# A fifth pair of a row by seven products, U1 summed in its PSUM bank, and the shared output added to x in DRAM

## What is computed

```
mlp(x, g, u, d) = (gelu(x @ g) * (x @ u)) @ d          # g, u: 256 x 1024, d: 1024 x 256
y = x + mlp(x, shared) + sum over the 2 chosen of 8 experts e: w[b, e] * mlp(x, skill[e])
out = y + y @ W_base.T + b_base + 2 * sum over e: cond[b, e] * (y @ A[e].T) @ B[e].T
```

## Time and profile before

| | us |
|---|---|
| median of 3 runs | 797.29 |
| lowest, highest | 796.95, 797.66 |
| the profiled execution | 796.85 |
| its span, first to last instruction | 795.0 |
| busy: TensorE (PE), its weight loads (PEld) | 789.5, 681.1 |
| busy: DVE, ACT, POOL | 668.8, 478.5, 278.4 |

### The profile page before, as it was taken

How to read it: one execution, slowest core, us unless ns; L and a number is a source line. 1 busy time by engine, 2 the same in 40 slices (tenths; PEclk the granted TensorE clock), 3 DMA queues, 4 the chain that set the end, 5 groups by cost and what they waited for, 6 DMA issues and landing times.

```text
span 795.0 us, 13413 instructions
## 1 busy us (share of the span) xinstructions
PE 789.5 (99%) x4133; PEld 681.1 (86%) x4133; DVE 668.8 (84%) x910; ACT 478.5 (60%) x737; POOL 278.4 (35%) x284
## 2 busy tenths in 40 slices
PE   8999999999999999999999999999999999999998
PEld 7888888888888888888888889888898888898887
DVE  4866888888887899889888898888898889889886
ACT  6554564564664666656666666666666666566653
POOL 1621321321430363263352444425435234532520
PEclk9999999999999999999999999999999999999999
DMA  7436506304726632563563275346336426631400
GB/s 204 123 80 200 144 1 198 121 1 146 233 72 206 222 116 80 171 184 101 165 189 95 90 224 153 105 141 189 106 125 215 124 80 198 172 108 51 133 2 27
DMA packets 138894, 105.21 MB, mean 132 GB/s; under 512 B 62928, under 2 KB 131280, under 8 KB 138832
## 3 DMA queue, kind: packets, MB, share of 16 engines
q1 hardware_dynamic: 138832, 104.53, 43.7%
HBM read 79.86 MB, written 24.64 MB: 131 GB/s over the span
## 4 chain that ended last, share of the span: by engine, by line
PE 99%; DMA 0%; DVE 0%; ACT 0%; SPq 0%; DVEq 0%; issue 0%
PE ps_ring L827 61%; PE ps_acc L827 36%; DMA raw<-_L_cond_shared_gate_dram 0%; PE ps_acc L1039 0%; PE ps_ring L848 0%; PE ps_ring L853 0%; PE ps_ring L857 0%; PE ps_acc L1059 0%; DVE stage L1925 0%; PE ps_acc L944 0%; PE ps_ring L1059 0%; ACT xc L1165 0%; PE ps_acc L1085 0%; ACT wide L1165 0%; SPq L517 0%
## 5 line engine op out<-in xcount | busy, mean ns | idle before, releaser
L827 PE MATMUL ps_ring<-xc,wide 128*128 128x512 f32 (+1 forms) x1926 | 416.2, 364 | 0.0
L827 PEld LDWEIGHTS ps_ring<-xc,wide 128*128 128x128 f32 x1926 | 336.8, 189 | 59.4 <-DVE post L1568 0.6
L1165 ACT CAST inner_hi<-post 128x512 fp32r<-128x512 f32 x192 | 117.7, 621 | 102.9 <-DVE post L1857 31.8
L827 PE MATMUL ps_acc<-inner_hi,wide 128*128 128x512 f32 x504 | 171.0, 390 | 0.0
L1511 DVE TENSOR_TENSOR inner_lo<-post,inner_hi 128x512 fp32r<-128x512 f32 x192 | 146.3, 769 | 9.0 <-ACT inner_hi L1165 6.1
L1168 ACT ACTIVATE post<-ps_ring 128x512 f32<-128x512 f32 (+1 forms) x125 | 68.0, 546 | 103.4 <-PE ps_ring L827 98.0
L827 PEld LDWEIGHTS ps_acc<-inner_hi,wide 128*128 128x128 f32 x504 | 94.8, 188 | 19.1
L827 PE MATMUL ps_acc<-inner_lo,wide 128*128 128x512 f32 x252 | 98.4, 391 | 0.0
L1168 ACT ACTIVATE post<-post 128x256 f32<-128x256 f32 (+1 forms) x98 | 53.7, 563 | 53.4 <-DVE post L1798 36.3
L827 PE MATMUL ps_acc<-inner_hi,sh_dn 128*128 128x512 f32 x256 | 83.9, 389 | 0.0
L1857 DVE SCALAR_TENSOR_TENSOR post<-post,coef_now,ps_ring 128x512 f32<-128x512 f32 x66 | 49.3, 747 | 36.2 <-PE ps_ring L827 34.1
(11 more groups left out here) (126 smaller groups left out, 1015.5 us busy)
## 6 DMA issues: line engine op xcount, KB each, us to landing
rights_scratch<-xc SPq DMA_DIRECT2D x6, 1792.0 KB, 10.2
raw<-n_L_cond_skill_gate_dram SPq DMA_DIRECT2D x32, 256.0 KB, 3.0
raw<-in_L_cond_skill_up_dram SPq DMA_DIRECT2D x32, 256.0 KB, 3.5
raw<-n_L_cond_skill_down_dram SPq DMA_DIRECT2D x32, 256.0 KB, 3.9
xbuf<-n_L_cond_skill_gate_dram SPq DMA_DIRECT2D x32, 256.0 KB, 3.0
xbuf<-in_L_cond_skill_up_dram SPq DMA_DIRECT2D x32, 256.0 KB, 3.5
xbuf<-n_L_cond_skill_down_dram SPq DMA_DIRECT2D x32, 256.0 KB, 3.8
xt_scratch<-xbuf SPq DMA_DIRECT2D x8, 512.0 KB, 3.3
```

The source lines that it names most:

```text
L827: last = pe.matmul(dst, left_[a], right_[b], start=start and n == 0, stop=stop and n == len(PASSES) - 1, skip_group_check=adds)
L1165: return nc.scalar.copy(dst, src)
```

## The change

- `SEVEN` becomes 1, 3, 5, 6, 7 and `FIRST_SEVEN` 3, 5, 6, 7: pairs 5, 6 and 7 stand next to one another.
- ACT copies bank 0 (P1) into bank 1, and the fourth product accumulates there; the finished U1 is copied to SBUF by ACT. DVE's addition at L1791 goes.
- For pairs by seven, block A21 of gate and up is not split any more (5/6 of the columns), the raw layout is regrouped for it. DVE's split of such a pair waits until POOL has read the slot.
- The `lo` parts of two steps are taken in one instruction where no pair by seven follows directly, else one by one within the next pair.
- x is stored to both `xt_scratch` and a new `base_scratch`; POOL adds the shared output to the latter with two accumulating transfers a quarter (`add_shared`). The row sum on POOL and SP's wait for it go. SP's loads and stores are reordered in a row.
- The orders by step are rewritten: down products of a pair behind a pair by seven go together after its second step, layer 1 is at step 5 in place of 4.
- Five transposes of the identity are added on TensorE between the first x transposes and the first unit.

```diff
...
-    L1_STEP = 4
+    L1_STEP = 5
     CONST_STEP = 3
     BW_STEP = 5
-    COEF_STEP = 13
+    COEF_STEP = 9
     FOLD_STEP = 8
     W_EFF_STEP = 9
-    W_EFF_FIRST_STEP = 10
-    W_EFF_LO_STEP = 12
+    W_EFF_LO_STEP = 2
     X_STEP = 8
-    TURN_STEP = 4
-    SEVEN = [1, 3, 5, 7]
+    LATE_STEP = 9
+    X1_LO_STEP = 4
+    TURN_STEP = 6
+    SEVEN = [1, 3, 5, 6, 7]
     FIRST_SEVEN = SEVEN[1:]
+    WHOLE_FIRST = len(SEVEN) - len(FIRST_SEVEN)
...
+        SPLIT_FIRST = {0: 2, 2: 3, 4: 4, 6: 5, 9: 6, 14: 9}
+        SPLIT_LATER = {1: 2, 4: 3, 5: 4, 6: 5, 9: 6, 14: 9}
+        SPLIT_WITHIN = {10: 7, 14: 8}
+        SPLIT_BEHIND = {10: 7}
+        SUMS_FIRST = {5: 1, 8: 2, 9: 3, 12: 4}
+        SUMS_LATER = {0: 0, 4: 1, 8: 2, 9: 3, 12: 4}
...
-                sp.dma_start(xt_dram[2 * qn + r], xbuf[:, r * 2 * S:(r + 1) * 2 * S]).then_inc(xt_stored[r], 16)
...
+                for to in (xt_dram, base_dram):
+                    sp.dma_start(to[2 * qn + r], xbuf[:, r * 2 * S:(r + 1) * 2 * S]).then_inc(xt_stored[r], 16)
...
+                    tokens(b)
+                    load_routed(b, 1, range(2, 3))
+                    sp.wait_ge(ex_s_made, 1)
+                    load_routed(b, 1, range(3, 4))
+                    load_routed(b + 1, 0, range(0, 2))
                 else:
+                    if not last:
+                        tokens(b)
+                    load_routed(b, 1, range(2, 3))
                     sp.wait_ge(x1_ready, b)
                     sp.wait_ge(sh_stored, 16 * B)
-                    sp.dma_start(base, sh_dram[b]).then_inc(base_landed, 16)
-                load_routed(b, 1, range(2, PAIRS))
+                    sp.dma_start(base, base_dram[b]).then_inc(base_landed, 16)
+                    load_routed(b, 1, range(3, 4))
+                    if not last:
+                        load_routed(b + 1, 0, range(0, 1))
+                    store_blocks(b - 1)
+                    if not last:
+                        load_routed(b + 1, 0, range(1, 2))
                 if not last:
-                    sp.wait_ge(base_ready, b + 1)
-                    sp.wait_ge(x_ready, b + 1)
-                    sp.dma_start(xf, xt_dram[b + 1]).then_inc(xf_landed, 16)
-                    load_routed(b + 1, 0, range(0, 1))
-                if not first:
-                    store_blocks(b - 1)
-                if not last:
-                    load_routed(b + 1, 0, range(1, PAIRS))
+                    load_routed(b + 1, 0, range(2, PAIRS))
                     load_routed(b + 1, 1, range(0, 2))
+            def tokens(b):
+                sp.wait_ge(x_ready, b + 1)
+                sp.dma_start(xf, xt_dram[b + 1]).then_inc(xf_landed, 16)
...
+            def add_shared(q):
+                for r in range(2):
+                    pool.wait_ge(xt_stored[r], 32 * (q + 1))
+                pool.wait_ge(acc0_out, 2 * (q + 1))
+                to, what = shared_place(q, 0)
+                pool.dma_start(to, what, accum_op=ALU.add).then_inc(sh_stored, 16)
+                pool.wait_ge(acc1_out, 2 * (q + 1))
+                to, what = shared_place(q, 1)
+                pool.dma_start(to, what, accum_op=ALU.add).then_inc(sh_stored, 16)
...
-                pool.wait_ge(weights_ready, b * (TOP_K * PAIRS) + (SEVEN[n_s - 1] + 1 if n_s else 0))
-                v = raw_gu(j).rearrange("p (g c i) -> p g c i", g=2, c=HC)
+                if not (b_first and SEVEN[n_s] == FIRST_SEVEN[0]):
+                    pool.wait_ge(ex_s_split, st)
...
             def row(b, first, last):
                 if first:
+                    add_shared(Q - 1)
                     pool.wait_ge(sh_stored, 16 * B)
-                    sums_of_weights(b, 1)
-                    row_sum(b)
-                    ex_c22(b, 1)
-                    sums_of_weights(b, 2)
+                    sums_of_weights(b, 1, True)
                 else:
                     sums_of_weights(b, 1)
                     ex_c22(b, 0)
-                    row_sum(b)
-                    sums_of_weights(b, 2)
-                    ex_c22(b, 1)
+                sums_of_weights(b, 2)
+                ex_c22(b, 1)
                 sums_of_weights(b, 3)
+                sums_of_weights(b, 4)
                 ex_c22(b, 2)
+                ex_c22(b, 3)
                 if not last:
                     sums_of_weights(b + 1, 0)
-                ex_c22(b, 3)
+                ex_c22(b, 4)
...
+            for _ in range(5):
+                pe.transpose(ring[3][:, 0:P], ident[:], ident[:])
...
+                    if n == 1:
+                        pe.wait_ge(ex_s_split, st + 1)
+                        if first:
+                            pe.wait_ge(ex_t_ready, 1)
+                    if n < 3 and k // 2 - 1 in sevens_of(first):
+                        pe.wait_ge([ex_mul, ex_c_done, ex_c_done][n], [3 * st - 2, 2 * st - 1, 2 * st][n])
+                    elif n == 0:
                         pe.wait_ge(gelu_done, whole(b, k - 1, first))
                     elif n == 1:
-                        if first:
-                            pe.wait_ge(ex_t_ready, 1)
                         pe.wait_ge(mul_done, whole(b, k - 1, first))
                     elif n == 2:
                         pe.wait_ge(mul_done, whole(b, k, first))
                     elif n == 3:
-                        pe.wait_ge(gelu_done, whole(b, k, first))
+                        pe.wait_ge(ex_copied, 2 * st + 1)
                     elif n in (4, 5):
                         pe.wait_ge(ex_copied, 2 * st + n - 3)
                     else:
                         pe.wait_ge(ex_v_done, st + 1)
                     for part in (GATE, UP):
                         last = product(ring[bank][:, part * HS:(part + 1) * HS],
-                                       [ex_left(n_s, hl, part, a_) for hl in range(2)],
+                                       [ex_left(par, n_s, hl, part, a_) for hl in range(2)],
                                        [ex_right(par, hl, b_) for hl in range(2)],
-                                       opens and part == GATE, True, True)
+                                       opens and part == GATE and n != 3, True, True)
...
-                    if k < 2 and not first:
-                        down(b - 1, K - 2 + k, False)
+                    if k == L1_STEP and not first:
+                        layer1(b - 1)
+                    if k == 1 and not first:
+                        down(b - 1, K - 2, False)
+                        down(b - 1, K - 1, False)
                     if k == 2:
                         pe.wait_ge(acc0_out, 2 * Q)
-                    if k >= 2:
+                    if k >= 2 and k // 2 - 1 not in sevens_of(first):
                         down(b, k - 2, first)
-                    if k == L1_STEP and not first:
-                        layer1(b - 1)
+                    elif k > 2 and k % 2 == 1:
+                        down(b, k - 3, first)
+                        down(b, k - 2, first)
...
+            def ex_copy_out(b, k, n_s, first):
                 st = seven_no(b, n_s)
+                behind_seven = k // 2 - 1 in sevens_of(first)
+                if behind_seven:
+                    ex_inner_hi_of(b, k - 2, n_s - 1, 0)
                 if first and SEVEN[n_s] == FIRST_SEVEN[0]:
                     act.wait_ge(turned_w, 1)
                     act.wait_ge(a_ready, 1)
-                elif n_s == 1:
+                act.wait_ge(ex_product, st * NP + 1)
+                if behind_seven:
+                    act.wait_ge(ex_u1_done, st)
+                else:
+                    act.wait_ge(gelu_done, whole(b, k, first))
+                nc.scalar.copy(ring[1][:], ring[0][:]).then_inc(ex_copied, 1)
+                if behind_seven:
+                    ex_inner_hi_of(b, k - 2, n_s - 1, 1)
+                act.wait_ge(ex_product, st * NP + 2)
+                act.wait_ge(ex_mul, 3 * st)
+                nc.scalar.copy(ex_v, ring[2][:]).then_inc(ex_copied, 1)
+            def ex_copy_u1(n_s, b):
+                st = seven_no(b, n_s)
+                if SEVEN[n_s] == L1_STEP // 2 + 1:
                     act.wait_ge(o_ready, b * 2)
-                for n, to, bank in ((0, ex_u1, 0), (1, ex_v, 2)):
-                    act.wait_ge(ex_product, st * NP + n + 1)
-                    if n == 0:
-                        act.wait_ge(ex_mul, 3 * st)
-                    nc.scalar.copy(to, ring[bank][:]).then_inc(ex_copied, 1)
+                act.wait_ge(ex_product, st * NP + 4)
+                nc.scalar.copy(ex_u1, ring[1][:]).then_inc(ex_u1_done, 1)
...
+            def split_routed(b, s, j, seven, first=False):
                 dve.wait_ge(weights_hi, b * (TOP_K * PAIRS) + PAIRS * s + j + 1)
-                last = take_lo(ex_all(1, j), raw[j], ex_all(0, j))
-                if not sums_follow:
-                    last.then_inc(weights_ready, 1)
+                if seven:
+                    if not first:
```

(33 more changed lines are left out.)

247 lines of the change are left out of this document (132 added, 115 removed).

## The result

The changed kernel takes **806.77 us** (median of four runs, 806.09 to 809.66), the kernel before took 797.35 beside it: a ratio of 1.0125 with a 95% interval of 1.010 to 1.0151, slower by 9.4 us. The forecast was 794.4. The profiled execution of the changed kernel is its longest, 809.66 us with a span of 807.8; the other three are 2.5 to 3.6 us shorter, so that the losses by place, which are read from this longest one, add up to more than those of the median.

What follows compares the result with a forecast made beforehand. TensorE's instruction count times pitch was taken as the bound, other engines hidden. Span 795.0 - 3.04 + 0.2 = 792.2, with 1.85 around it 794.0, plus 0.44 for the median: 794.4 us; range 793.3 to 797.6.

Steps and rivals of the forecast that it cites:

- rival B: Row 0 and shared quarters: accumulating transfers landing after 14 us lose 4 and 2 each, 804 us; decides from 12; chance 0.06.
- Eight pairs, 3.04 us: TensorE, one more pair by seven products in each row: eight pairs each 0.38 us shorter, 3.04 us off.
- E: Pairs by seven save nothing because narrow matmuls behind narrow ones wait for their weights: 797 us; chance 0.03.
- D: Columns alone set TensorE's pace, so narrow matmuls shrink with them: eight pairs save 5.4 us, 792 us; chance 0.02.
- Transposes 0: Kernel start: five more transposes fill TensorE's 0.6 us wait for the first x block; cost 0, bounds -0.1 to +0.1.
- U1 in its bank: ACT's copy into bank 1 takes 0.57 us, bounds to 1.3, ready 0.6 us before the fourth product; DVE's addition goes.
- Loads: Other engines' work in a row: DVE about -0.7 us from 59.1, ACT +4 from 42.8, POOL less; none near 66.8.
- The timetable: Adjacent pairs 5, 6, 7 and the next row's start: least slack 0.6 us, mostly 1.0; cost 0.
- C22 stands behind pair 7's sums: POOL's queue at pair 5: C22 ends at 6.9 us, pair 7's weights ready at 9.8, wanted at 15.5.
- Moved waits 0: SP's reordered stores and loads, DVE's pair 6 split waiting for POOL, layer 1 one step later: cost 0.
- Accumulating transfers 0: Shared output on POOL's queue: landing 4.5 to 9 us, against about 10 allowed in row 0 and 12 in quarters; cost 0.
- Plain stores at the start: Two x stores ahead of the third pair's shared weights delay them 3.4 us against 3.3 slack: 0.2 us, bounds 0 to 1.5.

Runs made afterwards that it cites:

- the repaired kernel: Changed kernel with plain SP stores, x added later in DRAM, ACT's and DVE's rows written out, no five transposes, C22 before pair 7's sums: 794.72 us.

## Why the prediction was wrong

The verdict went to rival B, the accumulating transfers, at 0.06, with a part that stood under no rival.

1. **Eight pairs, 3.04 us: right.** Rows of 66.83 to 66.85 where nothing waits, pairs of 7.77 to 7.79. Matmuls behind matmuls of 256 columns keep the 0.120 us of the earlier trace rows, so E and D fall, and with D the Trainium skill's 2.5 ns fixed part (TensorE: Matmul & The Clock Gate, section "Wait — 56ns, not 53.3ns?"), which this trace again does not show.
2. **Transposes 0: right** by the median; up to 0.64 in a profile.
3. **U1 in its bank: right.** The copy into PSUM took 0.57 to 0.58 us and was 0.6 ahead. What I did not see is how much it holds up (19 us).
4. **Loads: right in that none comes near the row's length.** In rows without waits DVE has 55.5 to 57.1 us of 66.85, where the sum gave 58.4, ACT 43.6 to 45.6 (46.8) and POOL 27.9 to 29.8 (26).
5. **The timetable: right inside the later rows, where TensorE waits for nothing, and incomplete in two ways.** I had written it for a later row and applied it to row 0, where pair 7's sums start 3.0 us into pair 5 and C22 behind them ends at 8.5: some 0.7 us lost, 0.4 of it given back by C22's earlier place, in the step "C22 stands behind pair 7's sums". And it took the row's beginning as step 14's remainder alone. It left out the turn of DVE's loop, which no wait of TensorE before named, because it was covered: DVE was idle there for 1.04 us at 453.32 (behind ACT's turn), while in the middle of the loop it was 0.50. With the row's work ending later, DVE's turn reaches pair 1's third product: 2.6 to 3.1 us over rows 3 and 5, and 4.9 in the profile of the changed kernel. **This was missed altogether.**
6. **Moved waits 0: half wrong.** I counted what stands in front of SP's stores and not what had stood behind the shared ones: 1.5 MB that now go out first and share the engines, 5 of the 13.2 us.
7. **Accumulating transfers 0: wrong, and the step that decided.** The bound "9 us, each byte read and written" was right for the median (8.0) and was taken for all places; in row 0 it was 13.2, past the 10 us of slack. There the wait and its clock cost 5.25 us. And in the quarters the test was wrong: I asked whether ACT would be kept waiting and found 12 us, but not what POOL's work would run beside once it was late. It ran beside DVE's, at 1.77 us for 0.68, and cost 3.8 us with the transfer well inside the slack. Even in row 0 the slack was less than I had it, for at 8.7 us TensorE already waited. Rival B's price (row 0: 4, three quarters: 2 each, 804) was close to the 5.25 and 3.8, its condition of 12 us too high: the quarter lost at 9.3. POOL's issues took 1.0 to 2.0 us as bounded, 0.55 to 0.94 when plain: it was not the issue that hurt but the landing. The Trainium skill (SBUF — State Buffer, section "SBUF: two separate sides") says that a POOL-issued transfer of 620 ns takes 3100 beside a copy of DVE, since its descriptors are not written while DVE holds the shared port. I had weighed this, and no run here shows how much of a landing is such a wait.
8. **Plain stores at the start: right in effect**, TensorE waited for nothing behind them. The working was off: 1 MB at 223 GB/s takes 4.7 us and not 3.4, and the weights' cast came 3.0 us later (29.20 for 26.23), 1.2 of it the late start of the kernel.

The range is also not what its bounds give: the small bounds for the better (0.2 and 0.1) lead from 794.4 to 794.1 and not to 793.3. Neither slip bears on the wrong forecast.

The sum holds when these are put right: 797.15 - 3.04 is 794.1, and the repaired kernel, which computes the same, stands at **794.72 us** (ratio 0.9970), with 0.24 us of the rest in row 0's pair 3 and 0.38 in its pair 6. It beats both kernels. What stays open is why DVE stands idle at its turn for 2.6 to 3.8 us in two pieces in the new order, where the old order showed 1 us, ended by ACT; it is shown that writing the loop out removes it, not what DVE waits for there.

## What to carry to other kernels

A transfer has a landing time for each place where it is waited for, and the median of the kernel is not it: look at what else is in the engines at that moment, and at what the old queue had held behind it. When a wait gets longer but stays inside its slack, ask what the delayed work will now run beside; DVE beside POOL took 1.8 us here for what takes 0.7 alone. And before slack at the end of a row is spent, look at the loop turn, for a gap that was covered leaves no wait in any list; writing out the loop of the one engine was enough here. And the accumulating transfers cost next to nothing once their source was in DRAM, nobody needed them soon, and their issue stood where POOL had no work waiting.

## What I had not expected of the hardware

- Accumulating 512 KB from SBUF into DRAM made three times the packets of a plain store (3456 for 1152), 2.4 times its time on the engines (3.3% for 1.4%) and landed in 8.0 us in place of 4.3; from DRAM to DRAM, eight of them landed in 6.2 (median; 7.2 in the repaired kernel).
- DVE at a turn of its loop in the new order: 1.7 to 1.9 us idle, and 0.9 to 2.05 more a few instructions later, where straight code has 0.2 and nothing; ACT's own turn cost nothing in the time.
- After a wait of 3.6 us in mid-kernel TensorE's granted clock was 0.50 for the next 3 us: 18 matmuls of 256 columns in 3.85 us, not 2.32, so the wait cost half as much again as its length. At row 3 of the changed kernel a wait of 1.6 us was followed by a clock of 0.52 for 3.3 us, and cost 3.7.
